# Tensor product of a graph network: rotated features and their scalar copy moved to the last two of nine steps

## The reference

```
R = relu(abs_distances[:, None] @ w1 + b1) @ w2 + b2      # radial weights, 384 per edge
Y = spherical_harmonics(rel_vec)
Fj = features[src]                                        # gather, 32 per edge
for i, (mo, lo) in enumerate(RS):                         # RS = [(8, 0), (8, 1)]
    acc = zeros((E, mo, 2 * lo + 1))
    for j, (mi, li) in enumerate(RS):
        for k, lf in enumerate(range(abs(lo - li), lo + li + 1)):
            acc = acc + NORM[i] * einsum('euv,ef,evi,ofi->euo', Rb[..., k], Yf, Fb, C)
out = zeros.at[dst].add(msg)
```

## Time and profile before

| | before |
|---|---|
| median of 3 runs | 12273.58 us (12273.4 to 12274.05) |
| profiled execution | 12262.02 us, its span 12256.3 us |
| busy share of the span: PE, PEld, DVE, ACT, POOL | 31%, 25%, 43%, 15%, 52% |
| gathers of `feat`, L969 | 3132, 947 ns each |
| products L1210 | 3132, 681 ns in the mean |
| `red` L1088 | 522, 421 ns each |
| `components` products L1181, reductions L1176 | 174 each, 1495 and 1625 ns |

### The profile page before, as it was taken

One profiled execution on the slowest core, in us unless ns is written; L12 is line 12 of the kernel. 1 busy time (PEld: TensorE's weight loads), 2 busy tenths in 40 slices (PEclk: granted clock), 3 DMA queues, 4 the chain that ended last, 5 costly groups with the idle time before them and its releaser, 6 DMA issues. The chain is left out here.

```text
span 12256.3 us, 73033 instructions
## 1 busy us (share of the span) xinstructions
PE 3840.2 (31%) x20408; PEld 3120.5 (25%) x20408; DVE 5220.4 (43%) x6900; ACT 1898.2 (15%) x1882; POOL 6351.7 (52%) x6677
## 2 busy tenths in 40 slices
PE   1000000000000000145555555464555555464544
PEld 0000000000000000034444444343444444343433
DVE  2233333333333334244544545454545445454544
ACT  0122222222222222000100101010100001010101
POOL 6766666666666666544444343434444443434343
PEclk5555555555555555577777777777777777777777
DMA  5333333434333434111111111111111111111111
GB/s 214 80 97 98 99 97 98 99 95 99 98 98 98 100 99 105 29 33 36 42 38 39 40 37 40 37 44 34 43 35 42 41 37 40 37 44 33 44 36 38
DMA packets 400152, 794.13 MB, mean 65 GB/s; under 512 B 164767, under 2 KB 242319, under 8 KB 388095
## 3 DMA queue, kind: packets, MB, share of 16 engines
q1 hardware_dynamic: 157528, 459.39, 14.0%
q0 software_dynamic: 213216, 166.16, 8.3%
q10 hardware_dynamic: 29382, 168.33, 3.4%
HBM read 499.75 MB, written 293.61 MB: 65 GB/s over the span
## 5 line engine op out<-in xcount | busy, mean ns | idle before, releaser
L969 POOL DMA_INDIRECT feat<-scratch_h,src x3132 | 2965.9, 947 | 3910.6 <-DMA src<-in_src 2973.0
L522 POOL DMA_INDIRECT kv<-scratch_kv,src_i x3132 | 2983.5, 953 | 1564.1 <-issue 973.4
L1210 DVE TENSOR_TENSOR prod<-psR,ops 128x384 f32<-128x384 f32 (+1 forms) x3132 | 1922.6, 681 | 3138.6 <-remote 2395.0
L995 PE MATMUL psS<-prod,ident 128*128 128x192 f32 x11136 | 2092.2, 348 | 2057.0 <-issue 1872.9
L995 PEld LDWEIGHTS psS<-prod,ident 128*128 128x128 f32 x11136 | 2018.8, 207 | 2144.0 <-issue 2116.8
L781 PE MATMUL psA<-ident,tail 128*36 128x128 f32 x3 | 0.8, 414 | 4553.0 <-DVEq L806 4553.0
L984 PE MATMUL psR<-whigh,stack 128*128 128x384 f16 x3132 | 1083.6, 347 | 452.8 <-issue 261.0
L1088 ACT ACTIVATE red<-psS,scales 128x192 f32<-128x192 f32 x522 | 219.9, 421 | 6071.6 <-remote 3522.0
L781 PEld LDWEIGHTS psA<-ident,tail 128*36 128x36 f32 x3 | 0.3, 129 | 4553.1 <-DVEq L806 4553.1
L985 PE MATMUL psR<-wlow,capped 128*128 128x384 f16 x3132 | 1082.7, 346 | 173.5 <-issue 172.9
L624 DVE TENSOR_TENSOR sq<-attr 128x162 f32<-128x162 f32 x58 | 19.0, 328 | 1870.9 <-DMA attr<-in_attr 1634.8
(11 more groups left out here) (253 smaller groups left out, 3875.2 us busy)
## 6 DMA issues: line engine op xcount, KB each, us to landing
w_row<-in_wT SPq DMA_DIRECT2D x232, 432.0 KB
stack<-scratch_hid SPq DMA_DIRECT2D x174, 576.0 KB
scratch_state<-out ACTq DMA_DIRECT2D x58, 1080.0 KB
scratch_qexp<-zeros ACTq DMA_DIRECT2D x32, 1566.0 KB
kv<-scratch_kv,src_i POOLq DMA_INDIRECT x3132
qin<-scratch_qexp SPq DMA_DIRECT2D x58, 864.0 KB
scratch_hid<-high SPq DMA_DIRECT2D x232, 216.0 KB
scratch_hid<-low SPq DMA_DIRECT2D x232, 216.0 KB
```

The source lines that it names most:

```text
L522: nc.gpsimd.indirect_dma_start(kv[b][:, t, :], None, a["kv"], bass.IndirectOffsetOnAxis(ap=src_i[b][:, t:t + 1].bitcast(U32), axis=0)).the ...
L969: nc.gpsimd.indirect_dma_start(feat[b][:, t, :], None, a["h2"], bass.IndirectOffsetOnAxis(ap=src_i[b][:, t:t + 1].bitcast(U32), axis=0)).t ...
L995: nc.tensor.matmul(psS[:, 0:GC].rearrange("p (t c) -> p t c", c=COLS), ident[:, :], prod[r][:, :, j, :], start=(n == 0), stop=False)
L1210: v.tensor_tensor(to[:, :, :, lo:lo + n], psR[:, g % 2, :, frm:frm + n * JC].rearrange("p t (j u) -> p t j u", j=JC), ops[b][:, ts, x * JC ...
```

## The change

VectorE's table `ahead` and ScalarE's list of cases are changed. The three `parts` products of the next chunk move from steps 5 and 6 to step 7; the two reductions of n = 3 move from step 7 to step 8, where n = 4 already was; ScalarE's scalar copy moves from behind `red` of step 5 to behind `red` of step 7, directly ahead of `turned`.

```
-                            if s == 5 and more:
+                            if s == 7 and more:
                                 scalars(1 - b, c + 1)
-                            if s == 7 and more:
                                 turned(1 - b, c + 1)
...
-                ahead = {5: (0,), 6: (1, 2), 7: (3,), 8: (4,)}
+                ahead = {7: (0, 1, 2), 8: (3, 4)}
```

## The result

The changed kernel takes 12399.6 us (median of 4 runs, 12392.5 to 12402.2), the kernel before 12273.5 us (median of 4, 12267.9 to 12274.1). The ratio is 1.0103, with a 95% interval of 1.0085 to 1.012: **slower by 1.0%, 126 us**. Forecast were 12379 us and a range of 12320 to 12428. In every comparison of this document two executions far longer than the others of their kernel are left out, one of e2's ten (10489 us) and one of n2's four (13753 us).

What follows compares the result with a forecast made beforehand. Gather and the stretch from its end to `red` of the next step 0 were taken to run in series; 28.15 - 26.31 = 1.84 us a chunk, 105 us in all, gave 12273.6 + 105 = 12379 us, range 12320 to 12428.

Steps and rivals of the forecast that it cites:

- What bounds the kernel: Each chunk's period, 119.6 us in one, is the gather plus the stretch from its end to `red` of next step 0.
- Steps 5 and 6 save nothing, VectorE waits for TensorE at step 7: 4.2 us of VectorE freed in steps 5 and 6 saves zero; VectorE waits at step 7, which gets down to 6.50.
- The new wait of 0.73 us: In step 8 VectorE's reductions wait 0.73 us for ScalarE's scalar copy behind `red` of step 7; bounds zero and 1.0.
- Three reductions, 4.76 to the fold: In step 8 three reductions take 4.84 us, less 0.08, before the fold, including 0.12 for a wait on VectorE's own counter.
- `red` of step 0 28.15 behind step 5: VectorE's chain through steps 7 and 8 puts next step 0's `red` 28.15 us behind that of step 5, 26.31 before.
- 1.84 us a chunk, 105 us: From `red` of step 5 to `red` of step 0, 28.15 - 26.31 = 1.84 us lost per chunk, 105 us in all.
- the falling clock: Rival: TensorE pauses in step 8 and the next drop its clock, two steps a chunk costing 640 us: 13020; chance 0.05.
- a sign named beforehand for being wrong: The forecast is wrong if TensorE's granted clock in steps 8 and 0 is below 1.00.
- Nothing past `red` of step 0: Behind `red` of step 0 VectorE's wait for the axes copy swallows the lateness; the gather finds the engines as before, no cost.
- TensorE's pace takes over: Rival: VectorE's chain from step 7 fits under TensorE, four steps take 25.04 us, 72 us less: 12201; chance 0.04.
- no change: Rival: a shifted period favours short step 4s, winning at best 0.8 of 1.84 us; 12331, or 12290 with free wait; chance 0.06.

Runs made afterwards that it cites:

- e2: Kernel before with only ScalarE's scalar copy moved from behind `red` of step 5 to behind that of step 6; ratio 0.9988 to the kernel before, engines not creeping.
- n2: Changed kernel without gathers from the third chunk on, scalar copy back behind `red` of step 5; median 8397.8 us, first to last `red` 3669.5 us.
- a1: Changed kernel unaltered, on a chip where engines do not creep under a gather; 8637.5 us against 8648.4 for the kernel before, ratio 0.9988.
- n5: Changed kernel without gathers from the third chunk on, the three `parts` products moved into step 8; median 9277.6 us, first to last `red` 3844.2 us.
- n1: Changed kernel with gathers left out from the third chunk on, features of two chunks reused; median 8469.7 us, first to last `red` 3741.9 us.
- n3: Changed kernel without gathers from the third chunk on, the three `parts` products back in steps 5 and 6; median 9176.2 us, first to last `red` 3747.5 us.
- n0: Kernel before with gathers left out from the third chunk on, features of two chunks reused; median 8319.4 us, first to last `red` 3592.0 us.
- e1: Changed kernel with ScalarE's scalar copy put back behind `red` of step 5, gathers kept; ratio 0.999 to the kernel before, engines not creeping.
- e4: Kernel before with the two reductions of step 7 moved to step 8, copy behind `red` of step 5; ratio 0.9986 to the kernel before, engines not creeping.

## Why the prediction was right, point by point

- **What bounds the kernel** (gather, then the stretch to `red` of step 0, in series): right for the chip of the comparison, and necessary for the result. a1 shows the opposite case: where gathers follow one another, the same edit costs nothing. The prediction took the creeping as given without a cause, which was enough for this chip; on the chip of a1 its 105 us would have been wrong, since the changed kernel there takes 11 us less than the kernel before.
- **Steps 5 and 6 save nothing, VectorE waits for TensorE at step 7**: right. The products start 0.98 us behind `red` of step 5 (said: 0.97), and step 7 takes 6.50.
- **The new wait of 0.73 us**: 0.75 shown, 42.3 us over 57 by the list of who waited for the copy. ScalarE started 0.32 behind `red`, as taken from `out`; VectorE woke 0.15 behind the copy's end rather than 0.04. n2 prices the wait at 0.83.
- **Three reductions, 4.76 to the fold**: 4.77 (8175.38 to 8180.15), with the own wait inside. The rule of the Trainium skill (VectorE: DVE Perf Modes, section "The DRAIN you can't avoid") that a semaphore between chained operations costs nothing would have changed 0.12 us a chunk. The trace does not bear the rule out for these instructions: two reductions overlap by 0.08 where nothing is waited for (8175.38 to 8177.02, the next from 8176.93), and the third starts 0.03 behind the end of the second, so 0.12 is lost again. Behind the three `parts` products of n5 VectorE stands idle 0.35.
- **`red` of step 0 28.15 behind step 5**: 28.27. The split was a little off, step 8 7.87 instead of about 7.6 and step 0 7.72 instead of about 7.8, and that the fold of step 8 doesn't decide, but the second half of the products does, is as said. Without the wait the prediction had 27.4; n2 measured 27.44.
- **1.84 us a chunk, 105 us**: the term that was too small. The chain gave 1.96, and **the clock** added 0.35 on top. I had the falling clock as a rival of its own, all or nothing at 640 us, with a chance of 0.05, and set it aside with the earlier trace rows, where it stood at 1.00 with TensorE busy 14.11 of 16.20 us. It came as a dip of about 0.8 us in 25 of 57 chunks. With that a sign named beforehand for being wrong appeared, a granted clock below 1.00 in steps 8 and 0: the chain was right, the step that left the clock out of it was not. The total stayed within the bounds by luck in this respect, since they had been set for a longer wait and a longer step 4, not for the clock. The earlier trace rows did not carry the argument. Its longest pause between matmuls is 0.65 us, that of steps 8 and 0 in the changed kernel 1.43; there TensorE is busy 12.87 of 15.5 us in the chunk shown. The Trainium skill, TensorE: Matmul & The Clock Gate, section "HAM oscillation — how this bites in real kernels", describes a drop at every wait for DMA between bursts of matmuls, waits longer than any pause here. The trace agrees in part only: the clock fell in 25 of 57 chunks, at pauses of 1.43 us, and cost 20 us in all, not 640. The prediction was right to expect no drop at every wait, and wrong to expect none at all.
- **Nothing past `red` of step 0**: right. The gap from `red` of step 0 to the gather stays at 2.8 us in the mean, and three copies are made under it as before (78.8 us from `red` of step 0 to that of step 3 in both, where a gather runs).
- The rivals "TensorE's pace takes over" and "no change" fall with the rows above on this kind of chip. The second is what a1 shows on another chip, by a mechanism it did not name.

## What to carry to other kernels

Where two engines feed each other through two buffers, moving work to a later step is free only up to the next point at which the other engine waits: follow one chain, instruction by instruction, from the last point where both are level to the event that starts the next period. Here that gave 28.15 us for a measured 28.27. Then ask whether the new pauses leave the clock as it was: the chain does not say so. A copy that another engine needs belongs behind the earliest event that permits it, not behind the one that is convenient in the code. And before a cost per chunk is multiplied by the chunks, ask what else sets the period: the same 2 us count in full, or not at all, by whether the gather stands in series or beside.

## What was not expected of the hardware

- The same kernel takes 12273, 12333, 8640 and 8648 us on four occasions, and what differs is whether the other engines creep while GpSimd gathers (119.5 us a chunk in the kernel before of the comparison, 68.4 in a1). With the gathers of this stage left out, n1 on one kind of chip and n3 on the other, which differ in where the three `parts` products stand, take 3741.9 and 3747.5 us from the first to the last `red`; no one kernel without gathers ran on both, but their steps 1 to 6 take the same. What holds the engines is open: the traces name no releaser ("remote", "issue"), and no run here was made to find it.
- TensorE's granted clock dips for a part of a step (0.80 in the mean over 8.6 us) although its longest pause in the two steps around it is 1.4 us. Over 57 chunks such dips come 25 times in the changed kernel, 30 in n1, 7 in n3 and 56 in n5, and never in steps 8 and 0 of the kernel before, nor in n0 or n2. The longest pause of TensorE in these two steps is 0.5 us in the kernel before and n0, 0.7 in n2, 1.4 in the changed kernel, n1 and n3, and 3.2 in n5. n3's chain is longer than n1's (28.67 against 28.27) and n3 dips less often, so the length of the chain alone does not decide. Why it takes some chunks and spares others was not tried.
- The changed kernel, and e1, e2 and e4, are 0.1% faster than the kernel before where the gather sets the pace. No trace of the kernel before was taken on such a chip, so this stays unexplained.
